# Block words, bias loads, two thirds of the edge sums and the order of the last chunks in a graph and attention kernel

## What is computed

```python
xn = layernorm(x)
# graph part: three kinds of edges, in this order: 256 (hh), 1280 (oo), 6656 (ho)
e_f   = relu(concat(xn[src], xn[dst]) @ W_kind + b_kind)        # 8192 x 1024
logit = e_f @ W_a + b_a
alpha = softmax of logit over the edges with the same dst
z_f   = segment_sum(alpha * xn[src], dst)                        # 512 x 1024
gnn   = relu(concat(xn, z_f) @ W_node + b_node)   # W_hn for 128 nodes, W_on for 384
# mixer: linear attention, 16 heads of 64, q and k through elu + 1
q, k, v = split(xn @ w_qkv + b_qkv)
mix   = (q @ (k^T v) / (q . sum(k))) @ w_proj + b_proj
x = x + gnn + mix
x = x + mlp(layernorm(x))         # 1024 -> 128 -> 1024, fake-quantised activations and weights
```

## Time and profile before

| | |
|---|---|
| median of three runs | 798.47 us (797.57 to 800.25) |
| the profiled execution | 795.88 us |
| its span, first to last instruction | 794.1 us |
| mean granted clock of TensorE | 0.904 |
| PE busy | 645.8 us (81% of the span) |
| VectorE busy | 533.2 us (67%) |
| ScalarE busy | 229.0 us (29%) |
| GpSimd busy | 221.3 us (28%) |

### The profile page before, as it was taken

How to read it: one execution, slowest core, us unless ns; L and a number is a source line. 1 busy time by engine, 2 the same in 40 slices (tenths; PEclk the granted TensorE clock), 3 DMA queues, 4 the chain that set the end, 5 groups by cost and what they waited for, 6 DMA issues and landing times.

```text
span 794.1 us, 8278 instructions
## 1 busy us (share of the span) xinstructions
PE 645.8 (81%) x2687; PEld 471.8 (59%) x2689; DVE 533.2 (67%) x1113; ACT 229.0 (29%) x294; POOL 221.3 (28%) x175
## 2 busy tenths in 40 slices
PE   4999999898786899599994747995966656798962
PEld 3888888786665688488862524784840111586621
DVE  7879533666387857567866596643578897327996
ACT  3344333223313424253331522323520010320101
POOL 3000335744365254655633242010000000002240
PEclk9999999999997899799997966998997779999895
DMA  8554649999989985998988398267450014140201
GB/s 346 213 199 158 252 151 341 366 364 340 295 278 367 363 270 175 335 326 251 362 268 221 97 292 253 85 226 267 156 182 17 1 53 159 51 129 18 106 27 80
DMA packets 43963, 167.54 MB, mean 211 GB/s; under 512 B 5392, under 2 KB 5776, under 8 KB 36752
## 3 DMA queue, kind: packets, MB, share of 16 engines
q1 hardware_dynamic: 23040, 93.01, 31.9%
q0 software_dynamic: 20160, 73.41, 30.2%
q10 hardware_dynamic: 720, 0.59, 0.2%
HBM read 150.21 MB, written 16.78 MB: 210 GB/s over the span
## 4 chain that ended last, share of the span: by engine, by line
PE 44%; DVE 27%; DMA 16%; issue 6%; ACT 4%; DVEq 2%; POOL 1%; SPq 0%; ACTq 0%; POOLq 0%
PE bank_low L1443 12%; PE bank_low L1444 11%; PE bank_low L1445 11%; DMA bias_bc<-in_bias_rows 7%; DVE w_lo L885 5%; DMA edge_tables<-stage 4%; DMA gathered_rows<-edge_tables,dst_row 2%; DVE gathered_rows L1059 2%; DMA w_raw<-in_wt 2%; DVE hot_src L1257 2%; DVEq L1038 2%; DVE hot_hi L1258 2%; PE bank_high L1601 1%; DVE hot_lo L1259 1%; DVE thrown_away L1181 1%
## 5 line engine op out<-in xcount | busy, mean ns | idle before, releaser
L1443 PE MATMUL bank_low<-w_hi,xT_hi 128*128 128x512 f32 x484 | 196.5, 406 | 34.6 <-ACT bank_low L684 24.6
L1444 PE MATMUL bank_low<-w_lo,xT_hi 128*128 128x512 f32 x484 | 193.9, 401 | 0.0
L1445 PE MATMUL bank_low<-w_hi,xT_lo 128*128 128x512 f32 x484 | 193.6, 400 | 0.0
L656 ACT ACTIVATE w_hi<-w_raw 128x2048 fp32r<-128x2048 f32 x49 | 93.8, 1913 | 173.0 <-PE bank_low L1445 95.0
L885 DVE TENSOR_TENSOR w_lo<-w_raw,w_hi 128x2048 fp32r<-128x2048 f32 x48 | 110.2, 2304 | 29.1 <-ACT w_hi L656 28.9
L1443 PEld LDWEIGHTS bank_low<-w_hi,xT_hi 128*128 128x128 f32 x484 | 94.4, 195 | 57.5 <-issue 29.2
L1059 DVE SCALAR_TENSOR_TENSOR gathered_rows<-gathered_rows,wa_bc 128x1024 f32<-128x1024 f32 x68 | 83.3, 1225 | 36.5 <-DMA gathered_rows<-edge_tables,dst_row 32.9
L1445 PEld LDWEIGHTS bank_low<-w_hi,xT_lo 128*128 128x128 f32 x484 | 94.2, 195 | 20.6
L1444 PEld LDWEIGHTS bank_low<-w_lo,xT_hi 128*128 128x128 f32 x484 | 94.6, 195 | 19.6
L587 POOL DMA_INDIRECT gathered_rows<-edge_tables,src_row x68 | 85.8, 1262 | 41.0 <-DMA edge_tables<-stage 20.6
L622 POOL TENSOR_TENSOR small<-small,nhalf 128x1 f32<-128x1 f32 x12 | 10.7, 890 | 244.1 <-DVE small L1337 231.2
(11 more groups left out here) (267 smaller groups left out, 961.1 us busy)
## 6 DMA issues: line engine op xcount, KB each, us to landing
w_raw<-in_wt SPq DMA_DIRECT2D x54, 1024.0 KB
edge_tables<-stage SPq DMA_DIRECT2D x32, 256.0 KB
bias_bc<-in_bias_rows SPq DMA_DIRECT2D x16, 256.0 KB
x_in<-in_x SPq DMA_DIRECT2D x4, 512.0 KB, 9.3
xn_scratch<-xn SPq DMA_DIRECT2D x4, 512.0 KB, 5.1
node_top<-stage SPq DMA_DIRECT2D x8, 256.0 KB
x_part<-in_x SPq DMA_DIRECT2D x8, 256.0 KB, 5.5
mix_out<-stage SPq DMA_DIRECT2D x8, 256.0 KB
```

The costliest lines, as they stand in the source:

```text
L656: act.activation(w_half(c, h)[0], raw[:, h, :], ACT.Copy).then_inc(w_hi_done, 1)
L1443: pe.matmul(dest, lh, rh, start=start and i == 0, stop=False, skip_group_check=True)
L1444: pe.matmul(dest, lh, rl, start=False, stop=False, skip_group_check=True)
L1445: last = pe.matmul(dest, ll, rh, start=False, stop=last_one, skip_group_check=True)
```

## The change

Four things are changed, and with them the places of some steps.

1. SP loads no bias rows any more. ScalarE issues the load of the next bias row itself, behind the last seed of the present one.
2. The block numbers of twelve tiles are packed into one number (two bits each), six words in all. VectorE reads them as two groups of three before the first tile and again before the second pass, TensorE once. Each use takes its two bits with a shift and a mask in registers. Thirteen small VectorE instructions are added at the start, and three where the places are read.
3. ON0 stands ahead of PR0. `ATTEND` and `DEN8` move: the first group's attention goes from Q1 to HN0 and ON0, the second group's from PR0 to ON0. `add_kq`, `hh_logits` and `split_feat` stand later in VectorE's order. `take_maxima` covers 24 tiles in PR1 and 32 in ON1 (before: 18 in ON0 and 18 in ON1), and the split of xn (`xn_hi`, `xn_lo`) moves from ON0 to ON1.
4. VectorE adds 45 of the 68 destination rows (`t % 3`), where it added 34.

```diff
-(HHT0, HHB0, HHT1, HHB1, K0, V0, K1, V1, Q0, Q1, HN0, PR0, PR1, HN1, ON0, ON1,
+(HHT0, HHB0, HHT1, HHB1, K0, V0, K1, V1, Q0, Q1, HN0, ON0, PR0, PR1, HN1, ON1,
  BON0, BON1, BHN0, BHN1) = range(TABLES, TABLES + 20)
...
-TILES = {4: (0, 1), 5: (3, 2), 6: (3, 2), 7: (2, 3), HHT0: (2, 1), HHB0: (1, 1), HHT1: (1, 2), HHB1: (1, 1),
-         K0: (3, 2), V0: (3, 2), K1: (3, 3), V1: (2, 3), Q0: (3, 2), Q1: (5, 2), HN0: (2, 0), PR0: (4, 3)}
+TILES = {4: (0, 1), 5: (2, 3), 6: (2, 3), 7: (2, 3), HHT0: (2, 1), HHB0: (1, 1), HHT1: (2, 1), HHB1: (1, 2),
+         K0: (3, 2), V0: (3, 2), K1: (4, 2), V1: (3, 2), Q0: (4, 2), Q1: (4, 2), HN0: (2, 0), ON0: (4, 2)}
-LAST_EDGES = PR0
-MAXIMA = {ON0: (0, 18), ON1: (18, 36)}
-T_EARLY = 36
+LAST_EDGES = ON0
+MAXIMA = {PR1: (0, 24), ON1: (24, 56)}
+T_EARLY = 56
...
-LOADED = 4
-ADDED_HERE = [t for t in range(T_GATHERED) if t % 2]
+PACKED = 12
+WORDS = (T_GATHERED + PACKED - 1) // PACKED
+ADDED_HERE = [t for t in range(T_GATHERED) if t % 3]
...
-ATTEND = {(Q1, 1, 0): [(0, 0), (0, 1)], (Q1, 1, 1): [(0, 2), (0, 3)], (PR0, 0, 1): [(1, 0), (1, 1)], (PR0, 0, 2): [(1, 2), (1, 3)]}
-DEN8 = {(Q1, 0, 2): 0, (HN0, 1, 0): 1}
+ATTEND = {(HN0, 1, 0): [(0, 0), (0, 1)], (ON0, 0, 0): [(0, 2), (0, 3)], (ON0, 1, 0): [(1, 0), (1, 1)], (ON0, 1, 2): [(1, 2), (1, 3)]}
+DEN8 = {(Q1, 1, 0): 0, (ON0, 0, 1): 1}
...
@@ SP
-            load_bias(c + 1)
@@ ScalarE, in seed()
                 act.activation(bank[bank_of[nc_, ni]][:, :], bias_bc[:, :], ACT.Copy).then_inc(seeded, 1)
+                if (nc_, ni) == seed_order[seeds_to(nc_ + 1) - 1] and nc_ != BIASED[-1]:
+                    act.wait_ge(seeded, seeds_to(nc_ + 1))
+                    load_bias(BIASED.index(nc_) + 1)
@@ ScalarE, the chunks
-            if c == PR0:
-                for j in range(4):
-                    attend(1, j)
-            if c == Q1:
-                for j in range(4):
-                    attend(0, j)
+                if (c, i) in ((HN0, 0), (ON0, 0), (ON0, 2)):
+                    a, j = int(c == ON0), 2 * int((c, i) == (ON0, 2))
+                    attend(a, j)
+                    attend(a, j + 1)
-            if c == ON0:
+            if c == ON1:
                 act.wait_ge(xnr_loaded, 16 * MT)
@@ VectorE, the block numbers
+        def load_blocks():
+
+            block_words.clear()
+            for first in range(0, WORDS, 3):
+                _, values = nc.values_load_multi_w_load_instructions(block_i[0:1, first:first + 3], engines=[mybir.EngineType.DVE],
+                                                                     min_val=0, max_val=4 ** PACKED - 1)
+                block_words.extend(values)
+
+        def block_of(t):
+
+            return (block_words[t // PACKED] >> (2 * (t % PACKED))) & (NB - 1)
 
         def edge_tile(t):
 
-            if t % LOADED == 0:
-                catch_up()
-                load_blocks(t)
@@ VectorE, the chunks
+            lo_half(c, 1)
+            if c == ON0:
+                for j in range(4):
+                    attend(0, j)
+            edge_work(c, 0)
             if c == HHT0:
                 split_feat(1)
-            lo_half(c, 1)
+            if c in (HHT1, K0):
+                for i in range(2):
+                    hh_logits(int(c == K0), i)
...
-            if c in (HHB0, HHB1):
-                for i in range(2):
-                    hh_logits(int(c == HHB1), i)
-            if c in (K0, K1):
-                for j in range(4):
-                    add_kq("k", int(c == K1), j)
```

More of the change, by code:

```diff
@@ L49 @@
 TABLES = 8
-(HHT0, HHB0, HHT1, HHB1, K0, V0, K1, V1, Q0, Q1, HN0, PR0, PR1, HN1, ON0, ON1,
+(HHT0, HHB0, HHT1, HHB1, K0, V0, K1, V1, Q0, Q1, HN0, ON0, PR0, PR1, HN1, ON1,
  BON0, BON1, BHN0, BHN1) = range(TABLES, TABLES + 20)
 CHUNKS = TABLES + 20
-WEIGHTS = [2, 3, 0, 1, 6, 7, 4, 5, 8, 9, 10, 11, 12, 14, 16, 17, 18, 19, 13, 22, 23, 15, 20, 21, 24, 25, 26, 27]
+WEIGHTS = [2, 3, 0, 1, 6, 7, 4, 5, 8, 9, 10, 11, 12, 14, 16, 17, 18, 19, 13, 20, 22, 23, 15, 21, 24, 25, 26, 27]
 BIAS_ROW = {2: 0, 3: 1, 6: 2, 7: 3, HHT0: 4, HHT1: 5, K0: 6, HN0: 7, V0: 8, HN1: 9, K1: 10, V1: 11, ON0: 12, ON1: 13, PR0: 14, PR1: 15}
 BIASED = sorted(BIAS_ROW)
-STORED = list(range(TABLES)) + [HN0, PR0, PR1, HN1, ON0, ON1]
+STORED = list(range(TABLES)) + [HN0, ON0, PR0, PR1, HN1, ON1]
 HH = (HHT0, HHB0, HHT1, HHB1)
@@ L747, in _ @@
                 split_feat(1)
+            if c == ON0:
+                for j in range(2, 4):
+                    attend(0, j)
             hi_half(c + 1, 0)
@@ L856, in _ @@
         dve.memset(seg_ends[:, 0:1], 0.0)
+        for i in range(PACKED):
+            dve.memset(weight4[:, i:i + 1], float(4 ** i))
         dve.memset(zeros[:, :], 0.0).then_inc(dve_consts, 1)
@@ L1121, in finish_hh @@
                 take_max(t)
+        load_blocks()
         dve.wait_ge(consts_ready, 5)
@@ L1200, in _ @@
                 dve.memset(vbuf[:, :, :, P:P + 1], 1.0).then_inc(kv_cleared, 1)
-            edge_work(c, 0)
+            if c in (V0, V1):
+                for j in range(4):
+                    add_kq("k", int(c == V1), j)
+            if c == Q1:
+                for j in range(4):
+                    add_kq("q", 0, j)
             if c == K1:
@@ L1205, in _ @@
                 spread_ks(1)
-            if c == Q1:
+            if c == HN0:
                 invert_den(0)
-            if c == PR0:
-                invert_den(1)
-            lo_half(c + 1, 0)
-            if c == Q1:
-                for j in range(4):
-                    attend(0, j)
             if c == PR0:
@@ L1216, in _ @@
                     attend(1, j)
-            edge_work(c, 1)
-            if c in (HHB0, HHB1):
-                for i in range(2):
-                    hh_logits(int(c == HHB1), i)
-            if c in (K0, K1):
-                for j in range(4):
-                    add_kq("k", int(c == K1), j)
-            if c in (Q0, Q1):
-                for j in range(4):
-                    add_kq("q", int(c == Q1), j)
+            if c == HN0:
+                for j in range(4):
+                    add_kq("q", 1, j)
+            lo_half(c + 1, 0)
+            if c == ON0:
+                invert_den(1)
+            edge_work(c, 1)
             if c in (PR0, PR1):
@@ L1628, in _ @@
             pe.matmul(bank[4 + s][:, :], zeros[:, :], iota[:, :], start=True, stop=True)
+        block_words = []
+        for first in range(0, WORDS, 3):
+            _, values = nc.values_load_multi_w_load_instructions(block_i[0:1, first:first + 3], engines=[mybir.EngineType.PE],
+                                                                 min_val=0, max_val=4 ** PACKED - 1)
+            block_words.extend(values)
         for t in range(T_GATHERED):
-            if t % LOADED == 0:
-                cols = block_i[0:1, t:t + LOADED]
-                _, block_of = nc.values_load_multi_w_load_instructions(cols, engines=[mybir.EngineType.PE], min_val=0, max_val=NB - 1)
-            out = bank_high[:, bass.ds(block_of[t % LOADED], 1), :].rearrange("p b n -> p (b n)")
+            block = (block_words[t // PACKED] >> (2 * (t % PACKED))) & (NB - 1)
+            out = bank_high[:, bass.ds(block, 1), :].rearrange("p b n -> p (b n)")
             pe.wait_ge(hot_done, 3 * (t + 1))
```

42 lines of the change are left out of this document (22 added, 20 removed).

## The result

The change made the kernel slower: 891.36 us (median; 886.09 to 892.55) against 798.02, a ratio of 1.116 with an interval of 1.111 to 1.121. The forecast was 749, its range 722 to 778, and "slower" had a chance of 0.04. The profiled execution has a span of 884.3 us and a mean granted clock of 0.864, where before it was 794.1 and 0.904.

What follows compares the result with a forecast made beforehand. TensorE's chunks were taken to set the pace, with idle waits between. Stretches −7 − 14 − 28 − 15 + 16 − 12 = −60, less 11 for gathers, gave −49: 746.9, 749 at the median, range 722 to 778.

Steps and rivals of the forecast that it cites:

- Two thirds of the sums: VectorE's edge tiles: 11 more adds, +13.4 us, within the 26 just freed and covered by idle time; 11 accumulating gathers fewer.
- The gathers bound the phase: Rival, gather phase: DMA share stays at 0.90 because GpSimd may run only three tiles ahead; 775 us, chance 0.22.
- Bias: TensorE's six waits for ScalarE's seeds: loading the next bias row earlier removes all, 34.1 us gross.
- Words: VectorE's block-number loads in the gather phase: 17 become 2, about 26 us of VectorE freed.
- A: Stretch of the last tables: two waits and the slow clock go, −7 us.
- B: Stretch of the hh chunks and K0: 66.4 us of work plus 12 of waits, 78.4 in all, −14 us.
- C: Stretch V0 to Q1: waits, half the attention and some clock loss go, 3 us of new wait, −28 us.
- D: Stretch HN0 and PR0, now with ON0: 92.8 us before, 78 forecast including 9 of new wait, −15 us.
- E: Stretch PR1 to ON1, without ON0: new waits in HN1 and ahead of the one-hot tiles, +16 us.
- F: Stretch of the one-hot tiles, set by VectorE: 5.9 us of loads and 20 picks go, −12 us.
- The register operations: Rival, VectorE and TensorE: 390 operations at 0.16 us each add 62 us, 811 us; chance 0.05, of which 0.04 slower.
- The bias row: Rival: ScalarE's load queues behind 1 MB of weights, so 34 us of waits stay; 783 us, chance 0.05.

Runs made afterwards that it cites:

- the kernel that took 768: The kernel after, two rows of three still added by VectorE, but GpSimd issues each tile's destination gather two tiles later: 767.75 us, ratio 0.962.
- adds undone, 780 us: The kernel after, but VectorE adds every second row again (34 of 68), with bias, words and order as in the change: 780.01 us, ratio 0.980.
- the mended one: The 768 us kernel with hh logits and key/query sums earlier, two tiles ahead of the second denominator, more picks in projection chunks: 748.83 us, 0.939.
- the bias run: The kernel before, with only the bias change: ScalarE issues the next bias row's load behind the present one's last seed, SP none: 776.63 us, 0.975.
- 759: The kernel after with every second row added, destination gathers in their old place, and the order of chunks and steps mended: 759.4 us, 0.950.
- the 767 of the old order: The kernel before with bias loads on ScalarE and packed words, old order, every second row added: 767.44 us, 0.962.

## Why the prediction was wrong

**The step that failed** is in "Two thirds of the sums": "GpSimd now runs less far ahead: a gather waits for the added tile two before, which was four tiles back and is now three". This follows the destination gathers alone, and prices the step by how many transfers it moves. What mattered stood behind them in the same stream. In the pattern of two the accumulating gather of tile 2k is issued behind a destination gather that waits for the add of tile 2k − 3: between that add and the use lie a dot product and two tiles, 1.2 + 1.85 + 3.07 = 6.1 us. In the pattern of three it is 1.2 us. (That counts the dot product alone. In the timeline above VectorE is ready at 335.11, 2.25 us after the add, and GpSimd issues 1.51 us after it, so 0.74 of the 8.56 us are covered and 7.82 waited.) Against the 8.56 us from issue to use, the one covers most, the other hardly anything. With that time the term would have been some 7 us for each of 23 gathers, 160 us, less what was hidden; in the forecast it was 0, beside 11 set aside for a phase mean. Measured: 111 us.

The same miss stands in the rivals. "The gathers bound the phase" had the right place (0.22) and the wrong mechanism: it went by DMA share 0.90, gave 26 us, and so ended at 775. The share fell to 0.74 up to the last tile; before, on the same stretch, it was 0.87. The sign named for it, waits for gathers "well over 36 us", showed (172.2). The other, "over 350 us" to the last tile, was ill chosen: the stretch to the last tile was 476.5 us here, but 359.6 in the kernel that took 768, since the 366 of the earlier trace rows ended before the last gather. To the last tile it was 401.8 before.

**Two terms that were too large.** Bias: 34.1 us of TensorE's waits were to go. Those for the row went, 22.2 us of TensorE's waits for seeds with them, and 15.0 came back ahead of the attention; alone it brought 20. Words: the 26 us were counted as cover for the 13.4 of adds, and not as what they also seem to have been, cover for gathers in flight; alone they brought 11.

**Where the rest lies.** The kernel of 768 us has the order of the change and early gathers, so its stretches, cut at the same matmuls, can be laid beside the forecast (us; the 11 for gathers stand beside the stretches, in none of them):

| | A | B | C | D | E | F |
|---|---|---|---|---|---|---|
| forecast | 56 | 78 | 123 | 78 | 69 | 71 |
| gathers two tiles later, 768 us | 56.1 | 94.9 | 130.6 | 77.1 | 74.3 | 73.3 |
| adds undone, 780 us | 56.1 | 95.7 | 143.5 | 72.1 | 75.5 | 72.9 |
| kernel after, 891 us | 67.0 | 126.6 | 189.9 | 91.4 | 74.1 | 73.5 |

A, D and F were right or nearly so. With early gathers the 19 us over the forecast are B (16), C (7), E (5) and F (2), less the 11; with the adds undone C is 20 over. The same rows for B and C, first of the kernel of 768 us, then of the mended one:

```profile
198.95:293.85 94.90, 73.08 (x307) 58.17 (x306) 79.73 (x120) 31.66 (x32) 52.02 (x37) 0.89 0.99 352
293.85:424.44 130.59, 123.95 (x553) 100.28 (x552) 102.52 (x160) 53.19 (x73) 74.82 (x57) 0.96 0.95 310
...
199.34:283.04 83.70, 72.69 (x307) 58.43 (x306) 74.43 (x109) 31.88 (x33) 51.17 (x34) 0.92 1.03 374
283.04:402.94 119.90, 119.90 (x553) 97.72 (x552) 97.18 (x158) 53.09 (x73) 77.50 (x55) 1.00 0.96 324
```

B had been given 66.4 us of work and 12 of waits, and nothing for the slow clock behind them. In the kernel of 768 us the waits were 19.1 (2.3, 6.0 and 10.9), and TensorE was busy for 73.1 us at a granted clock of 0.89. In the mended one they were 11.0, and 72.7 us at 0.92 are 67 at the full clock: the work was right, and about 6 us of clock were missing. Transfers are dense there too: the share is 0.99 and 1.03, and ScalarE waits 35.0 us for weights in B of the mended kernel. That they bound B isn't shown. The bytes that B moved before (316 GB/s for 92.26 us) would ask 372 GB/s in the 78.4 us forecast; those of the mended kernel, which are more, 399.

C took 119.9 in the mended kernel, all of it TensorE at 2.4 GHz, where 123 was forecast, so the sum of TensorE's work was sound. In the kernel of 768 us it waits there 2.4 us in V1 and 4.3 in Q1, behind the later sums of keys and queries, where 3 had been set; the mended order has these sums earlier and shows no such wait.

**What held.** The new waits, forecast and then measured in the kernel of 768 us, whose gathers are early: K0's bank 8 and 10.9; the second denominator 9 and 9.1; HN1's second half 10 and 11.5; ahead of the one-hot tiles 12.5 and 10.8. In the kernel after, those ahead of the last tile were longer (17.7 and 14.6), since the tiles ahead of them waited too; the last two were the same. F: about 71 forecast, 73.5 in the kernel after. The register operations, whose bound had reached 0.16 us each, cost 0.05 us for the two of a use: picks in the kernel after start 0.33 us apart, and before 0.28 (the one behind that of the earlier trace rows, 586.39, starts at 586.67):

```profile
645.02 0.35 DVE L1197 SCALAR_TENSOR_TENSOR other_node<-iota,dst_f,max_bc 128x128 bf16<-128x128 f16 x1
...
645.35 0.35 DVE L1197 SCALAR_TENSOR_TENSOR other_node<-iota,dst_f,max_bc 128x128 bf16<-128x128 f16 x1
```

The bias row was not late. By the rule that the prediction cited from the Trainium skill (DMA: Bandwidth & Descriptors, Issuing engines are not separate DMA queues), another issuing engine saves issue time only. The gain came mainly from the moment of issue, of which the rule says nothing: behind the seeds of HHT1 the bias run issued K0's row at 237.08 us, its last packet began at 243.62, and the first seed of K0 at 260.32. But the loads were also quicker. For the three issued between 230 and 290 us, the last packet began 9.3, 8.8 and 9.4 us after the issue before, and 6.5, 6.3 and 5.0 us in the bias run, where their packets have a queue apart from the weights'. Whether that queue or the traffic of the moment made the difference is open.

**The order** was forecast as a set of waits against larger gains, and as a whole it cost 12.6 us. What it bought, ON0 ahead of the projection and the attention later, shows only when its own waits are mended: 759 against the 767 of the old order.

Not settled: why 11 further adds cost 7 us, mostly in C, where VectorE's 13.4 us could have lain in its idle time, and how much of the excess in B and C goes to the bias and how much to the words.

## What to carry to other kernels

When one engine issues several kinds of transfers in order, price a change to one kind by what is queued behind its wait: for each transfer, name the event that lets it be issued, and count the work between that event and its use against the time from issue to use. A count of transfers and a bandwidth share tell nothing of that; here 11 accumulating gathers turned into plain ones, at a share that fell, made the kernel 111 us slower, and moving one block of the stream two tiles later took 124 us off. And before a stall is taken away, ask what it was covering.

## What had not been expected of the hardware

The traffic comes in bursts. While the accumulating gather of the timeline above was in flight, the DMA engines were nearly full (the columns are those of the stretches):

```profile
334.37:342.93 8.56, 8.46 (x38) 6.67 (x36) 0.58 (x4) 0.00 (x0) 3.47 (x3) 1.00 0.96 293
```

It was so at each of the 21 waits, shares of 0.89 to 1.05, though the means of B and C were 0.84 and 0.69: each add sets off several gathers at once, and the one that is needed lands among them (GpSimd itself issues nothing more until the next add). A low mean share is a sign of such rounds as much as of room. Two register operations ahead of an instruction cost 0.05 us together. And B of the mended kernel moved 374 GB/s over 83.7 us at a DMA share of 1.03; the page's slices of that kernel, 18.6 us each, reach 391.
